# A four-layer graph network on one core: the target sort moved under the edge scores, the last hop's rows stored in edge order, and one wide table of node rows

## The reference, cut to what matters

```python
x = _layernorm(x + L0(x, W_h, W_t, W_r, att_*, W_o, edge_index, edge_type))   # attention, 4 heads, 5 hops
x = _layernorm(x + L1(x, W, b, gamma, beta, 4))                              # GCN, 4 rounds with a norm in each
x = _layernorm(x + L2(x, edge_weight, W, bias))                              # Chebyshev, K = 3
x = _layernorm(x + L3(x, W_lin, b_lin, eps, W1, gamma, beta, W2))            # GIN with a batch norm
# L0: head_ids, tail_ids = src, dst
scores = leaky_relu(s_h + s_t + s_r)             # each: sum(tanh(row @ W) * att) of the edge's head, tail, relation
A = 0.9 * segment_softmax(scores, head_ids)
Z = x of every node, in 4 heads
for _ in range(5):
    Z = segment_sum(A * Z[tail_ids], head_ids) + 0.1 * x
out = Z.reshape(N, 4 * 64) @ W_o
# L1: loops added to the edges, deg over dst, norm = dis[src] * dis[dst]
for _ in range(4):
    agg = segment_sum((x @ W)[src] * norm, dst) + b
    x = (agg - mean) * rsqrt(var + EPS) * gamma + beta
# L2: deg = segment_sum(edge_weight, src); two propagations with -dinv[src]*w*dinv[dst], sums over src
# L3: sums of relu(h[dst]) over src, then a two-layer product with batch norm
```

## Time and profile before

| | us |
|---|---|
| median of three runs | 11303.64 |
| the profiled execution, from the first to the last instruction (span) | 11313.3 |
| sort, to the first one-hot product | 0 to 262 |
| histogram | 262 to 660 |
| node_degrees and plain_rows | 661 to 870, payload rows until 980 |
| round_weights, edge_fields | 980 to 1055 |
| edge_scores | 1055 to 2129 |
| edge_softmax | 2130 to 2231 |
| hops 0 to 3 | 2231, 2632, 3175, 3719 to 4262 |
| hop 4 (the last) | 4262 to 5360 |
| GCN rounds | 5371 to 8713 |
| Chebyshev, GIN | 8739 to 11313 |

### The profile page before, as it was taken

One profiled execution on the slowest core, in us unless ns is written; L12 is line 12 of the kernel. 1 busy time (PEld: TensorE's weight loads), 2 busy tenths in 40 slices (PEclk: granted clock), 3 DMA queues, 4 the chain that ended last, 5 costly groups with the idle time before them and its releaser, 6 DMA issues. The chain is left out here.

```text
span 11313.3 us, 114720 instructions
## 1 busy us (share of the span) xinstructions
PE 5814.6 (51%) x26903; PEld 4118.9 (36%) x26903; DVE 6720.9 (59%) x13563; ACT 2893.7 (26%) x5215; POOL 7596.6 (67%) x7480
## 2 busy tenths in 40 slices
PE   1762999500000005554777778677664558722245
PEld 1450322100000004554555566455553437622234
DVE  8982111495878784554667666687775766511127
ACT  0140222101222222222333344222221222200045
POOL 0755777687767676777767666676777767677730
PEclk9995999755555555565777777677776665555578
DMA  0461333263545452222776666565443999711158
GB/s 20 133 227 39 71 70 69 52 205 113 166 147 166 147 165 77 80 79 70 206 202 217 196 203 201 192 225 145 131 134 106 297 286 119 106 46 46 46 175 247
DMA packets 1425158, 1590.53 MB, mean 141 GB/s; under 512 B 994513, under 2 KB 1108527, under 8 KB 1424954
## 3 DMA queue, kind: packets, MB, share of 16 engines
q1 hardware_dynamic: 1145672, 1281.97, 35.9%
q0 software_dynamic: 264736, 260.68, 12.2%
q10 hardware_dynamic: 14546, 45.81, 1.0%
HBM read 908.86 MB, written 810.79 MB: 152 GB/s over the span
## 5 line engine op out<-in xcount | busy, mean ns | idle before, releaser
L2513 POOL DMA_INDIRECT r_got<-state,comb_src x1176 | 1182.6, 1006 | 442.9 <-issue 342.4
L334 POOL DMA_INDIRECT payload_or_bias_rows<-payload,place x700 | 786.9, 1124 | 547.9 <-POOLq L526 259.7
L1735 PE MATMUL hop_ps_into<-hop_out,span_s 128*128 128x256 f32 x8 | 4.9, 715 | 2032.9 <-DVE hop_out L1558 2032.9
L1366 POOL DMA_INDIRECT hop_got<-edges_b,next_col x784 | 801.3, 1022 | 262.0 <-issue 238.3
L1366 POOL DMA_INDIRECT hop_got<-edges_a,next_col x784 | 784.4, 1000 | 263.8 <-issue 238.2
L1735 PEld LDWEIGHTS hop_ps_into<-hop_out,span_s 128*128 128x128 f32 x8 | 2.0, 312 | 2035.1 <-DVE hop_out L1558 2035.1
L1623 ACT COPY hop_got<-hop_zeros 128x1792 f32<-128x1792 f32 x224 | 377.4, 1685 | 1391.6 <-DVE hop_ps_msg L1509 1117.4
L1558 DVE SCALAR_TENSOR_TENSOR hop_out<-hop_out,hop_runs_now,hop_ps_msg 128x256 f32<-128x256 f32 x1176 | 565.5, 481 | 50.9
L2803 PE MATMUL r_ps_v<-dense1g,r_gt 128*128 128x128 f32 x3136 | 589.5, 361 | 0.0
L2803 PEld LDWEIGHTS r_ps_v<-dense1g,r_gt 128*128 128x128 f32 x3136 | 535.0, 264 | 134.9 <-issue 134.9
L1135 DVE SCALAR_TENSOR_TENSOR sc_leaky<-sc_raw 4x896 f32<-4x896 f32 x56 | 60.4, 1079 | 825.0 <-ACT sc_raw L1109 825.0
(11 more groups left out here) (786 smaller groups left out, 18391.1 us busy)
## 6 DMA issues: line engine op xcount, KB each, us to landing
edges_a<-hop_out SPq DMA_DIRECT2D x112, 896.0 KB, 4.1
edges_b<-hop_out SPq DMA_DIRECT2D x112, 896.0 KB, 4.3
hop_side<-x_dst SPq DMA_DIRECT2D x280, 224.0 KB, 4.0
r_in<-state SPq DMA_DIRECT2D x112, 448.0 KB, 4.6
x_and_sums<-c_y SPq DMA_DIRECT2D x56, 896.0 KB
bn_in<-x_and_sums SPq DMA_DIRECT2D x56, 896.0 KB
r_own<-state SPq DMA_DIRECT2D x84, 448.0 KB, 5.9
g_rows<-r_gx SPq DMA_DIRECT2D x84, 448.0 KB, 2.6
```

What stands on the lines that cost most here:

```text
L334: nc.gpsimd.indirect_dma_start(out=rows[:, n - first, :], out_offset=None, in_=t.pay, in_offset=bass.IndirectOffsetOnAxis(t.place[:, k, n: ...
L1366: pool.indirect_dma_start(out=got[:, u, c, :], out_offset=None, in_=table, in_offset=at, bounds_check=EP - 1, oob_is_err=False).then_inc(g ...
L2513: pool.indirect_dma_start(out=got[:, n, c - b * CT, :], out_offset=None, in_=table, in_offset=bass.IndirectOffsetOnAxis(idx[:, at + c:at + ...
```

## The change

1. **The sort.** `sort_sources` sorts the sources alone: the same network over 512 keys per partition, an exchange is two operations over 256 columns, a turn 4 transposes. The targets get their keys inside `edge_scores` from the source-ordered edges, so the low bits of a target key are now a place in the source order. DVE does 8 key steps and the 136 exchanges there in 46 bodies, one body in each of the batches 1 to 46, at most `SORT_RATE` = 4 steps each. TensorE does the 4 transposes of a turn at the end of its batch, into a PSUM bank that the projections also use, and waits in its next batch, ahead of `project(1)`, until DVE has taken them. SP stores and reloads the sorted keys after body 46, and DVE reads them. A second payload table holds target, comb mark, row number.
2. **The tables.** `xe` and the 28 pieces under the histogram are gone. `node_degrees` writes three marks (dis, row number, comb) and `plain_rows` writes `nodes1`, 136 words per node: the 64 features, the three marks, the pad, then x and the row number. For that ScalarE makes one more copy of x per chunk; x is read into four buffers, and a chunk's buffers alternate as before. Both gathers of the scores read this table, 68 and 65 words at a stride of 136 words. From what they fetch DVE makes four small copies per batch (marks, row number, two of the payload).
3. **Payload rows.** Of the source order 240 stand in the histogram, 15 in `node_degrees`, 137 in `plain_rows`. Of the target order none stands in `plain_rows` or the scores any more: 14 in `target_fields`, 22 in `round_weights`, 22 in the degree scans, 44 in the softmax, 242 in hop 0, and 16 at the end of each of hops 1 to 3.
4. **Fields.** `edge_fields` is split: `source_fields` ahead of the scores; `target_fields`, `round_weights` and `edge_degrees` behind them.
5. **The last hop.** The scatters into `own1` and the 392 indices for them are gone. SP writes the row (now 68 words with its marks) in edge order behind the node rows of `own1`, in place of the write to `t.src[0]`.
6. **The rounds.** The rows of the last edges are found at 2 NP + edge place in `own1`, and at `SOURCES` + place in the state tables; `t.src` is gone. Node rows are read from `nodes1`, at a stride of 136 words in place of 68. Indices and mark columns change accordingly; `target_rows` computes two index arrays, and the first round no longer computes `t_row_s`.

```diff
 def sort_sources / order_keys
-                for b in range(1024 // P):
-                        ins = nc.tensor.transpose(out[:, b * P:(b + 1) * P], side(n)[:, b * P:(b + 1) * P], t.ident[:])
+def network_steps(nc, dve, order, turned, sides, taken, flip, across):
+    def exchange(split, d, given=None):
+        a, b = split(sides[c.n % 2] if given is None else given, d)
+        least, most = split(sides[(c.n + 1) % 2], d)
+        nc.vector.tensor_tensor(least, a, b, ALU.min)
+        c.link(nc.vector.tensor_tensor(most, a, b, ALU.max))
...
 def histogram
-                nc.scalar.copy(wide[:, m % 2, :, 0:D], narrow[:, m % 2]).then_inc(x_wide, 1)
-                act.dma_start(part(t.xe, m), wide[:, m % 2]).then_inc(x_out[m % 2], 16)
...
 def edge_scores
-                    for rows, by, cols in ((x, t.s_col, slice(0, D)), (t.xe, t.t_col, slice(D, 2 * D + 1))):
-                        pool.indirect_dma_start(out=got[:, u, c, cols], out_offset=None, in_=rows,
+                    for by, cols in ((t.s_col, slice(0, WS)), (t.t_col, slice(WS, WS + WT))):
+                        pool.indirect_dma_start(out=got[:, u, c, cols], out_offset=None, in_=flat,
...
-            payload_rows(nc, t, t.raw, 1, range(UNDER_SCORES), t.got_t)
...
+                if first_sort <= n < sort_end:                      # DVE
+                    for _ in islice(sorting, SORT_BODIES[n - first_sort][0]):
+                        pass
...
-                    nc.vector.tensor_copy(t.next_col[:, bass.ds((i * 2 + u) * CT, CT)], got[:, u, :, 2 * D]).then_inc(followed, 1)
+                    nc.vector.tensor_copy(t.marks_s[:, at, :], got[:, u, :, 0:4])
+                    nc.vector.tensor_copy(t.row_f[:, at], got[:, u, :, WS + D])
+                    nc.vector.tensor_copy(pay[:, j:j + CT, n * CT // HCOL, 1], got[:, u, :, 1])
+                    nc.vector.tensor_copy(pay[:, j:j + CT, n * CT // HCOL, 2], got[:, u, :, WS + D]).then_inc(followed, 1)
...
                     project(0)                                      # PE
+                    if turned_at:
+                        pe.wait_ge(order, turned_at + 1)
+                        turned_at = 0
                     project(1)
...
+                if first_sort <= n < sort_end and SORT_BODIES[n - first_sort][1]:
+                    turned_at, side = next(turns)
+                    pe.wait_ge(order, turned_at)
+                    for b in range(SPAN // P):
+                        ins = nc.tensor.transpose(psz[:, 1, 0, b * P:(b + 1) * P], (y, z)[side][:, b * P:(b + 1) * P], t.ident[:])
+                    ins.then_inc(sort_turned, 1)
...
 def edge_pass
-                    pool.wait_ge(y1_ready[u], i + 1)
-                    for c in range(CT):
-                        at = bass.IndirectOffsetOnAxis(put_flat[:, n * CT + c:n * CT + c + 1], 0)
-                        pool.indirect_dma_start(out=flat_rows, out_offset=at, in_=y1[:, u, c, :], in_offset=None).then_inc(stored[u], 16)
...
-                lag = (4 if turned else 2) if nodes else 0
+                lag = 2 if nodes else 0
...
+            if after is not None:
+                payload_rows(nc, t, 1, after, t.got_t)
...
-                            sp.dma_start(t.src[0].rearrange("(p j) w -> p j w", p=P)[:, bass.ds(order(i, u) * CT, CT), :],
-                                         y1[:, u, :, X1]).then_inc(y1_kept[u], 16)
+                            sp.dma_start(target[2 * NP:2 * NP + EP, :].rearrange("(p j) w -> p j w", p=P)[:, bass.ds(order(i, u) * CT, CT), :],
+                                         y1[:, u]).then_inc(y1_kept[u], 16)
...
-                        wait(dve, stored[u], i * per_store)
-                        nc.vector.tensor_scalar(y1[:, u, :, 0], t.negdinv_col[:, bass.ds(order(i, u) * CT, CT)], -1.0, None, ALU.mult)
+                        nc.vector.tensor_copy(y1[:, u, :, MARKS:ROW], t.marks_s[:, bass.ds(order(i, u) * CT, CT), :])
...
 def plain_rows
-                    sp.dma_start(chunk(t.own1, i, u, ROW), y[:, u]).then_inc(y_stored[u], 16)
+                    sp.dma_start(rows(t.nodes1, i, u, WIDE), y[:, u % 2]).then_inc(y_stored[u % 2], 16)
...
+                    nc.scalar.copy(y[:, u % 2, :, PLAIN:PLAIN + D], in0[:, u]).then_inc(x_copied[u % 2], 1)
...
-    t.own1 = dram("own1", [NP + EP, ROW])
-    t.src = [dram(f"source_rows{k}", [EP, D]) for k in range(4)]
-    t.state = [None] + [dram(f"state{k}", [NP + EP + P, D]) for k in (1, 2, 3)]
+    t.own1 = dram("own1", [2 * NP + EP, ROW])
+    t.nodes1 = t.own1[0:2 * NP].rearrange("(n k) w -> n (k w)", k=2)
+    t.state = [None] + [dram(f"state{k}", [SOURCES + EP, D]) for k in (1, 2, 3)]
```

## The result

The changed kernel took 11054.69 us (median of four runs, 11043.85 to 11064.29) against 11301.15 us for the kernel before in the same comparison: a ratio of 0.9779, 95% interval 0.9767 to 0.9791. It is 246 us faster. 411 us were forecast, and the stated range ended at 11025, so the forecast was wrong: right in direction, too large by 165 us.

What follows compares the result with a forecast made beforehand. It took DVE to bound sort and histogram, DMA most of `plain_rows`, POOL the scores and hops. Terms −95 + 1 − 35 + 32 + 85 + 6 + 18 − 428 + 5 = −411, from 11303.6 to 10893 us; range 10775 to 11025.

Steps and rivals of the forecast that it cites:

- Sort, −95: Source sort: exchanges over 256 columns save 71 us, turns 13, key steps and the rest about 11; together −95 us.
- `plain_rows`, −35: Stage `plain_rows`: fewer payload rows on POOL, transfers of 80.3 MB set the time, 263 us in place of 298.
- The slow bound: Upper end for `plain_rows`: transfers at 279 GB/s as before, 288 us, a gain of only 10 us.
- Fields, +32: Field, weight and degree stages: 58 payload rows moved in, 107 us in place of 75, +32 us.
- hops 0 to 3, +24: Hops 0 to 3: five more payload rows in hop 0, +6 us; sixteen each at the ends of hops 1 to 3, +18.
- Scores, +85: Edge scores: 272 sort operations of 0.35 us hold POOL for 0.85 of their time, 81 us, small copies 4; 1159 us.
- rival A: Edge scores: the sort is free under them, stage stays at 1074 us; sum −496, kernel 10808 us. Chance 0.20.
- Last hop, −428: Last hop: without 392 indirect DMAs, 11.3 us per batch; 670 us in place of 1098, −428 us.
- Rival E: Last hop: DVE and PE take turns, 22.3 us per batch, hop 1286 us (+188), kernel 11,509 us. Chance 0.03.
- Rounds, +5: Rounds: node rows read in 272-byte pieces at stride 544, less index computation; +5 us, from 0 to +40.
- Rival C: Wide table slow: +35 us in `plain_rows`, about 60 in the first round; together +95 to +100, kernel 10993 us. Chance 0.10.

Runs made afterwards that it cites:

- experiment 8: The changed kernel with four buffers in place of two for the wide rows that plain_rows stores: 11052.43 us, ratio 0.9773 to the kernel before.
- experiment 10: Changed kernel with last-hop squares ahead of the turned sum's copies, plus the first hop's 128x1792 multiply cut into seven of 128x256: 10694.33 us, ratio 0.9455.
- 11: Changed kernel with last-hop squares ahead of the turned sum's copies, plus the first hop's messages led through PSUM, multiply uncut: 10691.35 us, ratio 0.9455.
- experiment 6: The changed kernel with two extra SBUF maxima of 128x896 in each of the sort's 46 batches in the scores: scores 1151.2 us, +76.
- experiment 7: The changed kernel with the target sort's pieces moved behind the last batch of the scores: 11190.38 us, one run.
- experiment 5: The changed kernel with one extra SBUF maximum of 128x1792 in each of the sort's 46 batches in the scores, 92 us in all: scores 1163.4 us, +88.
- experiment 2: The kernel before with ScalarE's copy and squares of the batch two back moved ahead of the turned sum's copies in the last hop: 11296.98 us, ratio 0.9996.

## Why the prediction was wrong, by its own steps

*Sort, −95.* Measured −98. The line through two sizes gave 0.43 us for 256 elements and 0.80 us for an exchange; the trace after has 0.42 and 0.80 (76.97 to 77.77). Right.

```profile
76.97 0.42 DVE L355 TENSOR_TENSOR so_a<-so_taken 128x256 f32<-128x256 f32 x1
77.32 0.42 DVE L356 TENSOR_TENSOR so_a<-so_taken 128x256 f32<-128x256 f32 x1
77.77 0.43 DVE L355 TENSOR_TENSOR so_b<-so_a 128x256 f32<-128x256 f32 x1
```

*`plain_rows`, −35.* Measured −10, at the edge of its bounds. The slow bound, the rate as it was (279 GB/s), was the right one. I chose the middle on the ground that the loop is deeper; experiment 8 shows that depth doesn't change the rate.

*Fields, +32, and hops 0 to 3, +24.* Measured +37 and +24. Within the hops the parts were off against each other: the first hop got 17.5 us for its five rows and a changed end, the next three 6.3 us in all. Of the 6 us by which the payload rows delay each fix-up, most came back behind it, where POOL waits for the buffers to be cleared: 18.0 us before, 13.0 after.

*Scores, +85.* This step failed. The working took 0.85, the share of one 2.02 us multiply, over to 272 operations a fifth as long, as if POOL lost a fixed share of any such operation; the price of 0 stood only as the lower end and as rival A, at 0.20. (It also took 0.35 us for one operation where its own line in the sort's term gave 0.43; measured 0.42.) What POOL loses is the rest of the operation that a gather begins in (experiments 10 and 11), and of an unbroken run behind it (6): 13 us for the sort's 114, taken back at the one-hot (7). So the scores went as rival A said, with 0, but not for its reason: the short operations do not slip in between the gathers unnoticed.

The Trainium skill, page "SBUF — State Buffer", section "Who interferes with whom", gives the price of this change in the scores, 0, and for a reason that the runs do not bear out. It infers that a `tensor_tensor` does not hold up descriptor generation, which would make 0 of experiment 5's long operation and of the first hop's multiply too; the runs show 88 us for 92 us of the one, and 95 us of the first hop lost to the other. What the section says of two SBUF inputs agrees: with one input (and the output) in PSUM the effect was gone.

*Last hop, −428.* This step failed, and it is the larger part: −207 measured. 11.3 us per batch were taken from the busy times, DVE 10.5 and PE 10.9 to 12.2, as if the engines overlapped, with the argument that "the steps are those of different batches". For the products that is true. For ScalarE's squares it is not: in the rows that the argument used, DVE's reduction waits 5.49 us for ScalarE and PE's transposes wait 5.45 us for DVE. I read these as slack of a batch with time to spare. They were the two open ends of a ring; in the changed kernel they are still 5.4 us each, and it is the rest that became shorter; a batch takes 15.7 us. Rival E named turns between DVE and PE, with 22.3 us per batch; the truth, 15.7, lies between it and the forecast, since only part of each engine's work is in the ring. With the ring opened the hop came to 612 us from the fix-up to the row fix and DVE to 10.3 us per batch, so the estimate for DVE was good; PE's was too high (473 us busy, 8.5 per batch), since its granted clock, 0.81, was not the 0.51 of the like mix of products in the Chebyshev pass.

*Rounds, +5.* Measured −7: reading node rows at a stride of 544 bytes costs nothing (210 and 209 GB/s, 1054 and 1055 us). Rival C fell.

*The sum.* The last hop gained 221 us less than forecast, `plain_rows` 25 less and the fields 5 less; the scores cost 85 less, and the rounds and the small terms together 14 less. −411 became −259 in the profiled executions, and the scores' error hid more than a third of the last hop's: the result came as near as it did by luck.

## What to carry to other kernels

When the limiting engine is relieved, the next time per batch is not the largest busy time but the longest ring of waits; look for it before the change by following one batch's waits through each engine's order, and take a wait of several us on an engine that is not the limit as a part of such a ring until its releaser has been followed back. If an engine makes a late batch's step behind an early batch's, swap them: here it was worth more than the change itself, 297 us against 246, and nothing without it (experiment 2). Where GpSimd makes descriptors and is the limit, keep VectorE's operations with two SBUF inputs short and not back to back, or lead them through PSUM; and before pricing a new operation beside it, look which operation holds it already.

## What the runs showed of the hardware that was not expected

- GpSimd's making of the descriptors of one gather is held when it begins inside a VectorE operation with both inputs in SBUF: to 0.13 us before that operation's end (56 of 56 rows in the first hop, 0.69 to 1.84 us each), and not at all when it had begun before. As a share of VectorE's time that came to 0.27 for the second 272 operations of 0.42 us, 0.82 for pairs of 1.0 us and 0.95 for 2.0 us (0.31, 0.91 and 1.05 by the gathers alone), and 0 for 2.03 us with an input and the output in PSUM. The one-hot, a `tensor_scalar` of 0.7 us with a single tensor input, holds gathers too (56 of them by 19 us in experiment 7).
- Whether a held gather gets in at the border between two operations differs, and why is open. Behind the first of experiment 6's pair 37 of 45 stayed held through the second; between the seven pieces of experiment 10, 82 of 82 got in at the end of the piece that held them.
- The same 3081 matmul records of the last hop were 606 us busy at a granted clock of 0.62, and 473 us at 0.81, after a reordering on another engine had shortened PE's waits. In the kernel before, with the reordering and a batch of 19 us, they were 502 us at 0.67.
- Transfers of 448 KB in and 952 KB out per chunk ran at 277 to 283 GB/s with two or four buffers, as did the narrower ones of the kernel before.
